# A table of decays in a vision tower with a selective scan: turned by TensorE instead of by a transposing DMA

## What is computed

```python
h = patchify(x) @ W.T + b                       # 32 images, 36 tokens each, 768 -> 192
h = h + attn(layernorm(h))                      # rmsnorm, in/gate projection, selective scan, out, FFN
h = h + moe(layernorm(h))                       # 16 experts, top 4

def selective_scan(z, W_xproj, W_dt, b_dt, A_log, D_skip):
    xdbl = einsum('bld,kd->blk', z, W_xproj)
    dt_in, Bm, Cm = split(xdbl, [96, 112], axis=-1)
    dt = softplus(einsum('blr,dr->bld', dt_in, W_dt) + b_dt)
    A = -exp(A_log)                             # the table of decays: 384 channels x 16 states
    A_bar = exp(dt[..., None] * A)
    Bx = (dt * z)[..., None] * Bm[:, :, None, :]
    h = scan(h[t] = A_bar[t] * h[t-1] + Bx[t])
    return einsum('blds,bls->bld', h, Cm) + D_skip * z
```

## Time and profile before

| | before |
|---|---|
| median of 3 runs | 845.95 us (844.86 to 850.37) |
| the profiled execution's own time | 840.05 us |
| its span | 838.3 us |
| granted TensorE clock over the span | 0.871 of full |
| TensorE busy | 634.3 us (76%) |
| VectorE busy | 524.4 us (63%) |
| ScalarE busy | 274.8 us (33%) |
| POOL busy | 274.4 us (33%) |
| `decay_rows<-decay_log` in the chain that ended last | 5% of the span |

### The profile page before, as it was taken

The page is one execution under the profiler, slowest core; times in us unless marked ns, Lnnn a source line. Parts: engine busy times, 40 slices in busy tenths (PEclk is TensorE's granted clock), DMA queues, the critical chain, the costliest instruction groups (busy, mean ns, idle before and its releaser), DMA issues.

```text
span 838.3 us, 10285 instructions
## 1 busy us (share of the span) xinstructions
PE 634.3 (76%) x2852; PEld 464.0 (55%) x2852; DVE 524.4 (63%) x1104; ACT 274.8 (33%) x623; POOL 274.4 (33%) x266
## 2 busy tenths in 40 slices
PE   4027666766877878898877877998868688986996
PEld 3014443454765545675765545775755456765774
DVE  3003688734458988554568988554669987545664
ACT  0003754410264523121273432221373332212321
POOL 1023477721123545211214544111224454121321
PEclk9557677986986999998977999998968999997999
DMA  9996235522211011111211101122111101130440
GB/s 89 18 287 174 82 113 169 170 78 91 99 57 57 8 50 56 58 57 68 99 57 57 57 0 56 57 71 96 61 52 57 57 0 57 56 114 19 168 163 11
DMA packets 21137, 65.96 MB, mean 79 GB/s; under 512 B 8448, under 2 KB 13872, under 8 KB 15792
## 3 DMA queue, kind: packets, MB, share of 16 engines
q1 hardware_dynamic: 21088, 65.47, 29.2%
HBM read 55.15 MB, written 10.35 MB: 78 GB/s over the span
## 4 chain that ended last, share of the span: by engine, by line
PE 43%; DVE 25%; issue 12%; ACT 8%; DMA 6%; POOL 4%; DVEq 1%; SPq 0%; ACTq 0%; POOLq 0%
PE pa L488 25%; PE pb L488 18%; DVE state L976 9%; DMA decay_rows<-decay_log 5%; DVE pa L967 4%; DVE dt L952 4%; ACT scratch L745 3%; ACT a_bar L745 2%; POOL scratch L1217 2%; POOL root L1160 2%; DVE hid L1122 2%; ACT ffn L745 1%; DVE scratch L1113 1%; DMA decay<-decay_rows 1%; DVE scratch L1105 1%
## 5 line engine op out<-in xcount | busy, mean ns | idle before, releaser
L1205 POOL TENSOR_TENSOR read<-state,c_all 128x576 f32<-128x576 f32 x92 | 130.2, 1418 | 155.9 <-DVE state L976 149.9
L488 PE MATMUL pa<-bc_parts,pick_state 128*128 128x288 f32 x256 | 109.4, 470 | 90.7 <-DVE state L976 75.4
L1217 POOL TENSOR_TENSOR scratch<-scratch 128x288 f32<-128x288 f32 x96 | 77.2, 804 | 263.2 <-DVE scratch L1113 263.2
L488 PE MATMUL pb<-t_high,w 128*128 128x288 f32 x576 | 155.5, 335 | 4.0 <-DVE scratch L1097 3.9
L976 DVE TENSOR_TENSOR_SCAN state<-a_bar,pa 128x288 f32<-128x288 f32 x192 | 144.2, 751 | 16.0 <-ACT a_bar L745 0.5
L488 PEld LDWEIGHTS pa<-bc_parts,pick_state 128*128 128x128 f32 x256 | 57.5, 228 | 141.3 <-DVE state L976 115.6
L745 ACT ACTIVATE a_bar<-dt,decay 128x280 f32<-128x280 f32 x192 | 97.6, 524 | 112.6 <-DVE state L976 112.6
L488 PE MATMUL pa<-read,ident 128*128 128x288 f32 x384 | 126.2, 458 | 6.0 <-DVE read L984 5.8
L488 PEld LDWEIGHTS pb<-t_high,w 128*128 128x128 f32 x576 | 105.9, 198 | 18.5 <-DVE scratch L1097 6.1
L745 ACT ACTIVATE scratch<-pb,vec 128x288 f32<-128x288 f32 x96 | 48.0, 500 | 200.7 <-PE pb L488 200.7
L488 PE MATMUL pb<-t_low,w 128*128 128x288 f32 x384 | 111.6, 304 | 0.0
(11 more groups left out here) (130 smaller groups left out, 717.5 us busy)
## 6 DMA issues: line engine op xcount, KB each, us to landing
w<-w_store SPq DMA_DIRECT2D x32, 1152.0 KB, 5.1
w_store<-w SPq DMA_DIRECT2D x8, 1152.0 KB, 5.0
scratch<-expert_w SPq DMA_DIRECT2D x16, 384.0 KB, 5.6
x_patch<-patches SPq DMA_DIRECT2D x4, 864.0 KB, 4.5
w<-expert_w SPq DMA_DIRECT2D x1, 2304.0 KB, 13.8
x_patch<-patches SPq DMA_DIRECT2D x3, 288.0 KB, 4.2
w_embed<-embed_w SPq DMA_DIRECT2D x3, 256.0 KB, 3.6
hid<-unit_pick SPq DMA_DIRECT2D x1, 576.0 KB, 19.1
```

The costliest lines, as they stand in the source:

```text
L488: return nc.tensor.matmul(out, lhsT, rhs, start=start, stop=stop)
L1205: pool.tensor_tensor(read[:, i % READ_SLOTS, :], state[:, i % STATE_SLOTS, :], c_pair(i), ALU.mult)\
L1217: pool.tensor_tensor(glu, g_act, l_clip[un % 2], ALU.mult).then_inc(glu_ready.sem, 1)
```

## The change

The transposing DMA and the DRAM tensor go. `decay_log` is loaded as it lies, 128 rows of 192 bytes, into `raw_decay`, a free part of `result`, as a fourth of EMBED_LOADS. In `center` of chunk 0, TensorE transposes it with the identity into the free bank 0 of `pa`, behind the two matmuls of the mean. ScalarE takes the exponential out of PSUM into `decay_rows`, now an SBUF tensor of 48 x 128, behind its squares. SP then issues three DMAs from `decay_rows` into `decay`, one for each block of 128 channels, in 384 pieces of 64 bytes, and issues LATE_LOADS behind them. POOL waits for these three where it waited for the exponential, and TensorE's `scale` waits for the exponential, since it writes the bank.

```diff
+        decay_rows = sb("decay_rows", [NJ * GROUPS_PER_BLOCK, P])
...
-        decay_rows = nc.dram_tensor("decay_rows", [NJ * GROUPS_PER_BLOCK, P], F32).ap()
...
+        raw_decay = result[:, 1, 0:NJ * GROUPS_PER_BLOCK]
...
         EMBED_LOADS = ((vec[:, :], vectors), (mean_ones[:, :], ones_mean),
-                       (ident[:, :], identity))
+                       (ident[:, :], identity), (raw_decay, decay_log))
...
-            sp.dma_start(decay_rows, decay_log.rearrange("p g -> g p"), allow_slow_non_contiguous=True)\
-                .then_inc(decay_turned.sem, 16)
             for dst, src in SSM_LOADS:
                 sp.dma_start(dst, src).then_inc(load_ssm.sem, 16)
             for n in range(3):
                 load_raw(n)
+            sp.wait_ge(decay_exp.sem, 1)
+            for j in range(NJ):
+                sp.dma_start(decay[:, j, :], decay_rows[P // D8 * j:P // D8 * (j + 1), :]
+                             .rearrange("a (b n) -> a b n", n=STATES)).then_inc(load_decay.sem, 16)
             sp.wait_ge(constants.sem, 1)
-            sp.wait_ge(decay_turned.sem, 16)
-            sp.dma_start(decay[:, :, :], decay_rows.rearrange("(j a) (b n) -> (a b) j n", j=NJ, n=STATES))\
-                .then_inc(load_decay.sem, 16)
             for dst, src in LATE_LOADS:
...
                 feature_mean(2, h0, pe_mean)
+                if not after_first(c):
+
+                    nc.tensor.transpose(pa[0:NJ * GROUPS_PER_BLOCK, 0, 0:P], raw_decay, ident[:, :])\
+                        .then_inc(decay_turned.sem, 1)
...
             def scale(c, _):
+                if not after_first(c):
+                    pe.wait_ge(decay_exp.sem, 1)
                 spread_roots(c, 1, (0, 1))
...
                 activate(squares[:, :, :], centered[:, :, :], ACT.Square).then_inc(squared.sem, 1)
+                if not after_first(c):
+                    act.wait_ge(decay_turned.sem, 1)
+                    activate(decay_rows[:, :], pa[0:NJ * GROUPS_PER_BLOCK, 0, 0:P], ACT.Exp).then_inc(decay_exp.sem, 1)
...
-            act.wait_ge(load_decay.sem, 16)
-            activate(decay[:, :, :], decay[:, :, :], ACT.Exp).then_inc(decay_exp.sem, 1)
             act.wait_ge(load_embed.sem, 16 * len(EMBED_LOADS))
...
                 if not after_first(c):
-                    pool.wait_ge(decay_exp.sem, 1)
+                    pool.wait_ge(load_decay.sem, 16 * NJ)
                     pool.tensor_scalar(decay[:, :, :], decay[:, :, :], -1.0, None, ALU.mult)\
                         .then_inc(decay_ready.sem, 1)
```

## The result

| | before | with the change |
|---|---|---|
| median | 845.4 us (4 runs, 839.18 to 850.37) | 807.08 us (4 runs, 805.15 to 809.35) |
| the profiled execution, its span | 840.05, 838.3 | 805.15, 803.4 |
| granted TensorE clock | 0.871 | 0.881 |

The ratio is 0.9564, with a 95% interval of 0.9517 to 0.9611: the kernel is 38.3 us faster, where 41.0 was forecast, and 807.08 where 805 was. Of 845.4 us the interval is a gain of 32.9 to 40.8 us, so the 2.7 us between forecast and result are little more than the noise.

A forecast was written before the change was run, and what follows sets the result against it. It took the hole at the start, from the transposing DMA's small pieces and ScalarE's wait, as the bound. Terms -39.9 and -1.1 gave -41.0: 845.95 to 805 us, own range 802 to 809, wider range 798 to 813.

The forecast's parts named there:

- What bounds the kernel: Start: TensorE's hole, from ScalarE's wait for the table and the transposing DMA's 6144 pieces filling the DMA engines.
- First term: Start, embedding through ScalarE's table load: `h0` done at 14.15 instead of 54.08, -39.9 us.
- Second term: TensorE's four rows of the mean, after the embedding: 1.15 us at full pace instead of 2.27, -1.1 us.
- The thin stretch at half clock: TensorE's thinly used stretch after the mean: stays at 1.2 GHz as before; full-clock rival some 4.5 us more, chance 0.10.
- SSM_LOADS, transpose, moves, LATE_LOADS at 0: New waits after the start: each taken as 0 us; SSM_LOADS could cost 0 to 0.8, LATE_LOADS 0 to 2.
- The bound for the moves: SP's three moves of 384 pieces: at most the 8.59 us of the reading back, landing between 21 and 27.3.
- The late third pair: Rival at the embedding: third tile pair late by itself, -34.3 us, 812; chance 0.14 together with late loads pushing splits.
- The total: Whole kernel: -39.9 - 1.1 = -41.0 us, profiled execution 799.0, median 5.9 above it, 805 us.
- from there to the end I expect the order and the durations to stay: From 53.20, where ScalarE writes `h0`, to the end: all as before, 41.0 us earlier.
- The ranges: Whole kernel: own range 802 to 809 with chance 0.69; wider range 798 to 813 takes in full clock and late pair.

The follow-up runs named there:

- e1: Kernel before, with only ScalarE's exponential and its wait for the table moved behind the squares; transposing DMA kept: 837.03 us, ratio 0.9897.
- e2: Kernel with the change, plus the old transposing DMA in its old place, into a DRAM tensor nobody reads: 836.4 us, ratio 0.988.
- e4: Kernel with the change, ScalarE doing a one-column exponential at the front of its queue so its function tables load early: 802.9 us, ratio 0.9508.
- e5: Kernel with the change, plus 13 unused TensorE matmuls of 128x256 in the holes of the first chunk's start: 803.04 us, ratio 0.9503.
- e12: Kernel before, unaltered, profiled once more: 843.49 us, ratio 0.9993, span 836.2.
- e3: Kernel with the change, the wait for the exponential and the three moves put behind LATE_LOADS on SP: 808.04 us, ratio 0.9547.
- e10: Kernel with the change, ScalarE doing 4 extra copies of 144 columns ahead of `h0`: 808.2 us, ratio 0.9577.
- e11: Kernel with the change, ScalarE doing 6 extra copies of 144 columns ahead of `h0`: 809.17 us, ratio 0.96.
- e7: Kernel with the change, unaltered, profiled once more: 806.0 us, span 803.5.
- e6: Kernel with the change, plus early ScalarE tables, the 13 unused matmuls, and 12 warming matmuls ahead of the first data: 802.1 us, ratio 0.9485.
- e8: Kernel with the change, the old transposing DMA issued directly ahead of the three moves, into a tensor nobody reads: 827.55 us, ratio 0.9803.
- e9: Kernel with the change, ScalarE doing 2 extra copies of 144 columns ahead of `h0`: 807.51 us, ratio 0.9569.

## Why the prediction was right, point by point

- **What bounds the kernel.** Right. The hole was the start, and both of its causes counted: e1 gives 8.9 us for removing the wait and leaving the clog, where 60.56 - 52.2 was expected from the rows, and e2 takes 29 back with the clog alone.
- **First term, `h0` at 14.15.** It ended at 13.67. The embedding was through at 11.88 instead of 12.4, since its rows doubled their pace at 7.6 us here and at 8.2 in the profile of before, and the load of the tables was on the path as forecast (e4: 1.25, priced at 1.2). Against the profile of before that is -40.4 instead of -39.9.
- **Second term, the mean at full clock, -1.1.** Half right: 1.82 us instead of 1.15, since the clock fell within it. -0.45. Together `centered` came 40.86 us earlier, forecast 41.0; the two misses cancel, which is luck.
- **The thin stretch at half clock.** Right: 0.50 from 16 to 28 us. The Trainium skill, "TensorE: Matmul & The Clock Gate", "What's actually happening", has the throttled state as the default, which activity releases. These rows agree with it, and e5 shows the other side, 1.00 throughout with more to do. Up to 7.6 us the rows of the profile do not show it: the clock is given as 1.00 there though TensorE is at half pace (last section).
- **SSM_LOADS, transpose, moves, LATE_LOADS at 0.** Right. `w_dt` landed at 12.5 (forecast 12.1), POOL negated at 21.04, the patches landed at 41.0 (bound 45.7), and at 129.48 the shift is still 41.03. The bound for the moves, 8.59 us, was far too high: 1.9 each. The row had belonged to a transfer behind a full queue. The Trainium skill, "DMA: Bandwidth & Descriptors", gives under "Specifications" 512 bytes as the least size for line rate; in these 24 KB in pieces of 64 bytes nothing of it is seen on the path.
- **The late third pair.** That rival did not come: TensorE did not wait. With the transposing DMA behind the pairs the wait was 4.34 us before, 1.70 in e12 and none in e1 and e2; in the ten profiles without it there, none. So the forecast was right to put it down to that DMA, as far as fourteen profiles tell, and how much it costs differs by execution.
- **The total, -41.0 against -38.3.** The time of 805 for 807.08 comes of two misses that nearly cancel. The profiled execution was to take 799.0 us and took 805.15, 6.1 more; and its median was to lie 5.9 over it, as before, and lies 1.9 over it. That is luck. All but 0.1 us of the 6.1 is lost after the start: the step "from there to the end I expect the order and the durations to stay" holds for the order, not for the durations (next point). And "at 53.20 ScalarE writes `h0`" is a time of one execution, not of the kernel: in e12 it was 49.51, and from there the start gains 52.92 - 15.75 = 37.2 us, not 40.9. How often which length of the hole occurs is open: two profiles don't tell it.
- **Between the two profiles, 41.0 became 34.9.** This happens after the start, in steps, the largest, 4.1 us, between the fourth and the fifth row of the table. It need not come with the change. This is that stretch in the kernel before, in e4 (the kernel with the change, tables early), in the kernel with the change and in e3, columns as in rows 5:

```profile
347.65:742.62 394.97, 328.97 (x1556) 246.17 (x1556) 271.24 (x582) 134.00 (x308) 123.02 (x112) 0.92 0.17 60
307.49:702.42 394.93, 328.94 (x1556) 246.17 (x1556) 271.17 (x582) 134.01 (x308) 122.70 (x112) 0.92 0.17 60
307.75:706.78 399.03, 332.95 (x1556) 249.74 (x1556) 270.69 (x582) 133.93 (x308) 122.70 (x112) 0.91 0.17 59
308.13:710.55 402.42, 337.36 (x1556) 252.76 (x1556) 271.18 (x582) 134.00 (x308) 122.68 (x112) 0.89 0.17 59
```

The counts are the same in all four, and so, within 0.6 us, is the work of VectorE, ScalarE and POOL. TensorE's alone grows, by 4.0 and 8.4 us, at a lower mean clock (third number from the end), and the stretch by 4.1 and 7.5. With the change, e4 goes through it as fast as the kernel before, and set against e12 it keeps its whole gain: `centered` is 38.2 us earlier and the span, 798.1 against 836.2, is 38.1 shorter. Over all fourteen profiles the stretch has one of four lengths: 394.9 us (before, e12, e1, e4), 397.3 (e10, e11), 398.9 to 399.1 (after, e7, e6, e8, e9) and 402.4 to 402.5 (e2, e3, e5). The same holds for whole executions: of e12's ten, the three with spans of 836.2 to 837.2 us have a granted clock of 0.871, the six over 841 have 0.852 to 0.860. So the steps are time that TensorE spends at the lower clock, and the profiles of before and e12, both at 0.871, were quick executions by it. What decides which course of the clock an execution gets is open; the shifts of e9 to e11 were meant to find it and don't. Nor is it excluded that the change makes a slower course more frequent: of the eleven profiles with the change, e4's alone has the shortest stretch, and all three without it have.
- **The ranges.** "802 to 809" does not follow from its own terms: 805 with a spread of -1.1 to +4.4 and waits of 0 to 2.8 gives 804 to 812. The stated range, 798 to 813, was wide enough for either.

## What to carry to other kernels

When a wait for a slow DMA heads the list, ask what else was issued behind it: here removing the wait gave 9 us and removing the DMA that filled the queue another 29. Moving the DMA was no way out in the place that was tried: behind the loads of the start, with the table's moves behind it, it cost 20.5 us (e8). Issuing it from another engine's queue was not tried. A time taken from one profile of a transfer of thousands of small pieces is good to some us only; profile the kernel before twice before a forecast that rests on it. Look, too, at the granted clock of every execution: a difference of a few us between two profiles can be the clock's course and not the change. When a first instruction is moved away from the front of an engine's queue, look at what it carried, such as the load of the function tables.

## What the runs showed of the hardware beyond that

- 6144 pieces of 4 bytes took 37.10 and 39.38 us in two executions of the same kernel, and between 37.3 and 39.8 in e1, e2 and e8. Three DMAs of 128 pieces of 64 bytes took 1.9 us each to land on a queue that was free, and 14.3 behind LATE_LOADS (e3).
- SP can hang in the issue of one DMA because of another ahead of it: 14.80 to 20.42 us for `w_in`, behind the transposing one (e12, e1, e2, before), against 0.43 without it.
- The embedding's 24 rows took 7.68, 8.36, 8.45 and 7.81 us in four kernels with the same code there (after, e4, e5, e3), all at a granted clock that the profile gives as 1.00. The pace of the rows says otherwise. In the kernel with the change they start 0.48 us apart up to 7.24 us, which is the pace of the last eight rows before, at 0.50 of the clock, and 0.24 apart from 7.59 on; in e4 and e5 the step comes at 9.1, in e3 at 8.0. So the first seven to ten rows ran at the pace of 1.2 GHz, and where the step falls makes the difference. The kernel with the change, with 4 and then 9 rows in 2 us:

```profile
4.00:6.00 2.00, 1.80 (x4) 1.37 (x5) 1.92 (x1) 0.00 (x0) 0.00 (x0) 1.00 0.99 361
8.00:10.00 2.00, 2.00 (x9) 1.55 (x9) 2.00 (x1) 0.00 (x0) 0.00 (x0) 1.00 1.05 266
```

- The single executions of one kernel lay 1.6 (e5) to 11 us (before) apart. The medians of four runs in e9 to e11 came within 0.6 us of the shift of `centered` in their profiles, which is closer than their intervals of some 4 us let one expect.
